# Gate of 16 columns in four column groups, keys first, and new orders in modulated and chunk attention

## Chip, cores and metric

The kernel runs as one program on one core of a Trainium2 chip. The metric is the device time of one execution in microseconds (us), lower is better. Three runs of the kernel before took 3989.94, 3992.09 and 3993.36 us; the median is 3992.09.

## The reference, cut to what matters

The reference is a stack of two layers with layer normalization after each of four sublayers, on 4 x 1024 tokens of 256 features. The change touches two of them. The first attention has 16 heads of 16 features, and a gate per token and head that multiplies the scores:

```python
q = (hidden_states @ Wq + bq)      # 16 heads of 16 features; k and v alike
scores = einsum('bhqd,bhkd->bhqk', q, k) / sqrt(HD)
mod = sigmoid(hidden_states @ cg_W + cg_b + (cons_vec @ am_W + am_b))   # cg_W is 256 x 16
scores = scores * mod.transpose(0, 2, 1)[..., None]
probs = softmax(scores, axis=-1)
```

Beside it a second attention with 4 heads of 64 features is computed from the same tokens (q2, k2, v2). The attention of the second layer works in chunks of 64 tokens: causal softmax attention inside a chunk, plus 0.1 times the queries against a memory matrix per head that earlier chunks have written:

```python
scores = einsum('bhid,bhjd->bhij', qi, ki) * scale      # 16 heads, 64 x 64 a chunk
attn = softmax(where(mask, -inf, scores), axis=-1)
chunk_out = einsum('bhij,bhjd->bhid', attn, vi) + 0.1 * einsum('bhid,bhde->bhie', qi, M)
```

The rest (a third attention, two mixtures of experts, the memory updates) is not touched.

## The kernel before, in words

The stages run one after another, each in a block of its own with one instruction stream per engine: TensorE (PE), VectorE (DVE), ScalarE (ACT), GpSimd (POOL) and SyncE (SP, which issues most transfers). Streams meet only at semaphores. Within a stage the order of each engine is written out by hand.

**First projections**, `project_hidden`. Eight chunks of 512 tokens, two to a pass of the loop (j = 0, 1). The jobs of a chunk are a list: the gate in two tiles of 128 rows, queries and keys in two each, q2 and k2 in two each, values in four. Each job is a product into one of seven PSUM banks, taken in turn; before job n TensorE waits until the bank of job n - 7 has been emptied. For the gate the 16 columns of the weights are repeated 16 times on the host, so that the product has the gate on each of the 256 rows of the queries (`cg_W16`, `am_W16`). ScalarE empties the banks of the gate (L347, sigmoid), the keys (L358), q2 and k2 (L352). VectorE empties the queries with the gate multiplied in (L383), splits queries and keys into three bf16 parts each (`split_exactly`, L206 and L209), and empties the values (L389, L390). SP stores the parts, queries ahead of keys (L295), then q2 and k2 (L299) and the values (L302, L303). GpSimd loads the next tokens (L404). ScalarE issues the loads of the last group of weights before its loop (L188).

**Modulated attention**, `quad_attention`. 16 groups of four heads and one batch, each in two halves of 512 queries, each half in eight units of 128 keys. TensorE computes the scores twice: once ahead (12 units ahead), for the maxima, into a ring of three banks that VectorE reduces (L533, L626), and once for the exponentials (L554), to which the negated maximum is added through rows of the query operand. For that VectorE makes per half a `shift` of two bf16 parts (`make_shift`: L633, L636, L638, each needing the one before), TensorE turns it through a bank of the ring (`turn_shift`, L540), ScalarE copies it (`copy_shift`, L593) and GpSimd places it by transfer (L684). The fourth user after a turn of the same bank waits for the copy. The unit's order on TensorE and ScalarE is

```python
maxima(u + AHEAD, 0); values(u - LAG); maxima(u + AHEAD, 1)
for i in range(2): scores(u, i)
if u in turns: turn_shift(turns[u])          # TensorE
for i in range(2): activation(..., Exp)      # ScalarE, L610
if u in turns: copy_shift(turns[u])
```

`values` (L563) multiplies the exponentials with the values, in four column groups of 32.

**Chunk attention**, `chunk_attention`. 32 tiles of 128 tokens (two chunks), four to an iteration, software-pipelined: at step t TensorE does the scores of tile t (L2561 adds the causal mask, L2565), the output product of tile t - 4 (L2573), the turned probabilities of t - 1 (L2579), the context of t - 2 (L2591 memory part, L2594 values part), and turns the output of t - 8 (L2603). For the scores GpSimd expands the keys (L2539): for each chunk and half of the features eight copies, each blank but for one head's rows. VectorE takes the maximum (L2676), subtracts it (L2678), sums the exponentials of t - 1 (L2668), inverts (L2670) and multiplies (L2673), adds the residual (L2693), takes statistics (L2695, L2697), and once in four tiles writes four tiles of output (L2686). ScalarE takes the exponential (L2623), copies the turned probabilities (L2620), the context (L2628) and the turned output (L2631), and lays out the values (L2639). Expanded keys, scores and probabilities have two buffers each, the turned probabilities one bank pair in PSUM.

## Time and profile before

| | |
|---|---|
| median of three runs | 3992.09 us |
| profiled execution, own time | 3997.91 us |
| its span | 3996.2 us |
| mean granted TensorE clock | 0.938 of full speed |
| TensorE busy | 3580.1 us (90%) |
| VectorE busy | 2339.2 us (59%) |
| ScalarE busy | 1502.5 us (38%) |
| GpSimd busy | 1540.2 us (39%) |
| DMA | 366.44 MB, mean 92 GB/s |

Busy shares are means over stages with different limits. The profile's numbers are of one execution, 5.8 us above the median. A clock of 1.00 is 2.4 GHz, 0.50 is 1.2 GHz. A float32 product shows as two records of its shape. PEld rows are loads of weights, PE rows the products; products are pipelined, so that a row's own time is longer than its distance to the next.

### The profile page before, as it was taken

The numbers are of one execution on the slowest core, as the hardware profiler recorded it, in microseconds if no ns is written. First come the engines' busy times: TensorE is split into PE (matmuls) and PEld (weight loads), VectorE is DVE, ScalarE is ACT, GpSimd is POOL, SyncE is SP. The second block draws the span as 40 slices with busy tenths as digits, with TensorE's granted clock in tenths as the row PEclk, the third lists the DMA queues.
The fourth block names the chain that finished last, engine by engine and source line by source line (L and its number), as shares of the span: only waits on it lengthen the run. The fifth ranks groups of instructions, "written<-read, shape, count | busy, mean of one in ns | idle before, by whom it ended". The sixth has DMA issues, their size and how long they took to land. (4 is left out here: it accounts for less than half of the span.)

```text
span 3996.2 us, 55438 instructions
## 1 busy us (share of the span) xinstructions
PE 3580.1 (90%) x19176; PEld 1710.4 (43%) x19176; DVE 2339.2 (59%) x3916; ACT 1502.5 (38%) x2216; POOL 1540.2 (39%) x1343
## 2 busy tenths in 40 slices
PE   9989999997999889998789656687998989999995
PEld 4412222222333343333545355443554655655653
DVE  5679999994666326664632458977896631111112
ACT  2237777775444323444222334212553211111112
POOL 0142222222788505887346323144552322222221
PEclk9979999998999999999889766899999989999998
DMA  5622222221112151120622421454442123333333
GB/s 182 209 77 68 76 62 62 69 71 48 36 47 63 58 195 58 43 81 16 187 71 85 150 70 45 164 127 109 131 136 83 34 69 91 103 101 105 100 90 95
DMA packets 309775, 366.44 MB, mean 92 GB/s; under 512 B 54130, under 2 KB 241796, under 8 KB 308548
## 3 DMA queue, kind: packets, MB, share of 16 engines
q1 hardware_dynamic: 269972, 305.81, 24.4%
q0 software_dynamic: 30384, 50.90, 5.5%
q10 hardware_dynamic: 9216, 7.09, 0.6%
q8 instruction: 120, 1.97, 0.2%
q14 instruction: 83, 0.68, 0.1%
HBM read 228.00 MB, written 127.27 MB: 89 GB/s over the span
## 5 line engine op out<-in xcount | busy, mean ns | idle before, releaser
L626 DVE TENSOR_REDUCE modulated_mx<-modulated_ring 128x1 f32<-128x512 f32 x1024 | 651.8, 683 | 43.1 <-PE modulated_ring L533 37.4
L610 ACT ACTIVATE modulated_probs<-modulated_scores 128x1024 f32<-128x1024 f32 x512 | 496.1, 1021 | 189.1 <-PE modulated_scores L554 189.0
L3234 DVE TENSOR_TENSOR expert_h<-expert_gelu,expert_bank 128x512 f32<-128x512 f32 x128 | 88.0, 688 | 390.9 <-PE expert_bank L3163 385.4
L3205 ACT ACTIVATE expert_gelu<-expert_bank 128x512 f32<-128x512 f32 x128 | 76.4, 597 | 549.4 <-PE expert_bank L3163 546.5
L3123 POOL DMA_INDIRECT scratch_acc<-expert_y,expert_idx x64 | 100.8, 1575 | 427.5 <-DVE expert_y L3239 404.2
L1019 POOL TENSOR_TENSOR causal_total<-causal_total,causal_probs 128x1024 f32<-128x1024 f32 x96 | 227.1, 2366 | 59.1 <-ACT causal_probs L928 51.7
L1019 POOL TENSOR_TENSOR meta_total<-meta_total,meta_probs 128x1024 f32<-128x1024 f32 x96 | 227.1, 2366 | 58.7 <-ACT meta_probs L928 51.3
L950 DVE TENSOR_REDUCE meta_mx<-meta_maxima 128x2 f32<-128x1024 f32 x120 | 146.9, 1224 | 117.7 <-PE meta_maxima L815 117.1
L950 DVE TENSOR_REDUCE causal_mx<-causal_maxima 128x2 f32<-128x1024 f32 x120 | 146.9, 1224 | 117.7 <-PE causal_maxima L815 117.1
L928 ACT ACTIVATE meta_probs<-meta_scores 128x1024 f32<-128x1024 f32 x128 | 131.0, 1024 | 142.2 <-PE meta_scores L841 139.3
L928 ACT ACTIVATE causal_probs<-causal_scores 128x1024 f32<-128x1024 f32 x128 | 131.0, 1024 | 142.1 <-PE causal_scores L841 139.1
L2539 POOL TENSOR_TENSOR chunk_kexp<-chunk_kT,chunk_blocks 128x512 f32<-128x512 f32 x128 | 138.3, 1112 | 91.8 <-PE chunk_scores L2565 90.9
L563 PE MATMUL modulated_acc<-modulated_probs,modulated_v 128*32 128x512 f32 x1280 | 170.5, 605 | 0.0
L554 PE MATMUL modulated_scores<-modulated_q,modulated_k 128*128 128x512 bf16 x640 | 166.0, 382 | 1.2 <-DMA modulated_q<-modulated_turned 1.2
L1505 PE MATMUL top_ups<-top_wgu,top_xT 128*128 x284 | 142.2, 624 | 2.1 <-ACT top_xT L1553 1.7
L533 PE MATMUL modulated_ring<-modulated_k,modulated_q 64*128 64x512 bf16 x640 | 137.4, 387 | 6.5 <-ACT modulated_turned L593 5.9
L3239 DVE TENSOR_SCALAR expert_y<-expert_bank,chosen_weights 128x256 f32<-128x256 f32 x64 | 31.0, 484 | 188.5 <-PE expert_bank L3160 188.5
L533 PEld LDWEIGHTS modulated_ring<-modulated_k,modulated_q 64*128 64x128 bf16 x640 | 34.2, 92 | 212.5 <-DVE modulated_mx L626 181.7
L3163 PE MATMUL expert_bank<-expert_xT,first_wg 128*128 128x512 f32 x256 | 122.3, 600 | 2.7 <-DVEq L64 1.6
L3163 PE MATMUL expert_bank<-expert_xT,first_wu 128*128 128x512 f32 x256 | 121.4, 597 | 0.0
L3163 PE MATMUL expert_bank<-expert_xT,expert_wg 128*128 128x512 f32 x256 | 120.4, 592 | 1.0 <-DVE expert_h L3234 1.0
L3163 PE MATMUL expert_bank<-expert_xT,expert_wu 128*128 128x512 f32 x256 | 120.3, 592 | 0.0
(546 smaller groups left out, 7521.2 us busy)
## 6 DMA issues: line engine op xcount, KB each, us to landing
scratch_v<-proj_v SPq DMA_DIRECT2D x8, 1024.0 KB, 6.8
ahead_ctx<-scratch_ctx SPq DMA_DIRECT2D x16, 512.0 KB, 4.7
scratch_M<-steps_snap SPq DMA_DIRECT2D x16, 512.0 KB, 3.3
chunk_raw_v<-scratch_v SPq DMA_DIRECT2D x64, 128.0 KB, 2.8
chunk_mem<-scratch_M SPq DMA_DIRECT2D x32, 256.0 KB, 3.0
first_wg<-x_WgT SPq DMA_DIRECT2D x8, 1024.0 KB, 5.0
first_wu<-x_WuT SPq DMA_DIRECT2D x8, 1024.0 KB, 7.1
first_wd<-x_WdT SPq DMA_DIRECT2D x8, 1024.0 KB, 6.8
```

The lines of the kernel that those rows point to most:

```text
L533: nc.tensor.matmul(ring[bank_of["max", 4 * m + j]][:], qs[s][first(j), place(j), t * P:(t + 1) * P], ks[s][first(j), place(j), keys * CH:( ...
L554: last = nc.tensor.matmul(sc[i][:, x, :], ks[s][:, o, t * P:(t + 1) * P], qs[s][:, o, half * CH:(half + 1) * CH], start=True, stop=True)
L563: last = nc.tensor.matmul(acc[32 * j:32 * j + 32, :], vs[g % SLOTS][:, t, j, :], probs[u % NPROBS][j // 2][:, j % 2, :], start=(t == 0), s ...
L610: nc.scalar.activation(probs[u % NPROBS][i][:], sc[i][:], ACT.Exp, scale=SCALE).then_inc(s_exp, 1)
L626: V.tensor_reduce(mx[h % 2][:, x // 2, 1 - j % 2, j // 2, x % 2:x % 2 + 1], ring[bank_of["max", 4 * m + j]][:], AX.X, ALU.max).then_inc(s_ ...
L928: nc.scalar.activation(probs[u % NPROBS][:], sc[u % 2][:], ACT.Exp, scale=SCALE).then_inc(s_exp, 1)
L950: V.tensor_reduce(mx[g % 2][:, x // 2, :, x % 2], maxima_at(m)[:], AX.X, ALU.max).then_inc(s_red, 1)
L1019: G.tensor_tensor(total[g % 2][:], total[g % 2][:], probs[u % NPROBS][:], ALU.add).then_inc(s_add, 1)
L1505: last = nc.tensor.matmul(ups[i % 2][:], xT[i % 2][:, kd, :], wgu[:, kd, bass.ds(e, 1), :].rearrange("p e n -> p (e n)"), start=(kd == 0), ...
L2539: ins = G.tensor_tensor(kexp[j % 2][:, c, h], kT[j][:, h, c * C64:(c + 1) * C64].unsqueeze(1).broadcast_to([P, HP, C64]), blocks[:].unsque ...
L3123: added[j].done(G.indirect_dma_start(out=scr["acc"], out_offset=bass.IndirectOffsetOnAxis(ap=idx[j][a][:], axis=0), in_=y[j][:, a, :], in_ ...
L3163: last = nc.tensor.matmul(out[:], (wg if kind == "g" else wu)[j][:, kd, m * P:(m + 1) * P], xT[j][:, kd, :], start=(kd == 0), stop=(kd == ...
```

## The change

In the projections the gate becomes one job a chunk, on 32 columns (the 16 twice): four column groups of the array each take a quarter of the chunk's 512 tokens. ScalarE takes one sigmoid of 128 x 128 and issues eight transfers that lay each head's row on the 16 rows of its features. The keys come ahead of the queries.

```diff
-        T_KINDS = ("mod", "q", "k", "q2", "k2")
+        T_KINDS = ("k", "q", "q2", "k2")
+        GROUPS, WIDE = 4, P // 4
...
-        kinds = [(x, m) for x in T_KINDS for m in range(KD)] + [("v", t) for t in range(TT)]
+        kinds = [("gate", 0)] + [(x, m) for x in T_KINDS for m in range(KD)] + [("v", t) for t in range(TT)]
...
+                    if kind == "gate":
+                        for kd in range(KD):
+                            for r in range(GROUPS):
+                                toks = slice(r * (CH // GROUPS), (r + 1) * (CH // GROUPS))
+                                last = nc.tensor.matmul(bank[n % BANKS][r * WIDE:(r + 1) * WIDE, 0:CH // GROUPS], wg[:, kd, :], xT[j][:, kd, toks],
+                                                        start=(kd == 0), stop=(kd == KD - 1))
...
-                    if kind == "mod":
-                        dve_s.wait(act, i, (1 - j, "q", m), back=1 - j)
-                        ins = nc.scalar.activation(mod[:, m, :], bank[n % BANKS][:], ACT.Sigmoid, bias=modb[:, m:m + 1])
+                    if kind == "gate":
...
+                        act_s.done(nc.scalar.activation(gate[:], bank[n % BANKS][:, 0:CH // GROUPS], ACT.Sigmoid, bias=modb[:]), job)
+                        act_s.wait(act, i, job)
+                        dve_s.wait(act, i, (1 - j, "q", KD - 1), back=1 - j)
+                        for r in range(GROUPS):
+                            for c in range(KD):
+                                first = r * WIDE + c * (P // HD16)
+                                mod_laid[j].done(act.dma_start(mod[:, c, r * (CH // GROUPS):(r + 1) * (CH // GROUPS)],
+                                                               gate[first:first + P // HD16, :].unsqueeze(1).broadcast_to([P // HD16, HD16, CH // GROUPS])))
+                        continue
...
-                        act_s.wait(dve, i, (j, "mod", m))
+                        if m == 0:
+                            mod_laid[j].wait(dve, i)
```

In modulated attention the turned shift goes ahead of the unit's scores on TensorE, its copy ahead of the exponentials on ScalarE, and the three operations of `make_shift` go between the reductions of the unit that follows.

```diff
+                if u in turns:
+                    turn_shift(turns[u])
                 for i in range(2):
                     scores(u, i)
-                if u in turns:
-                    turn_shift(turns[u])
...
+                if u in turns:
+                    copy_shift(turns[u])
                 for i in range(2):
                     act.wait_ge(s_sc, 2 * u + i + 1)
...
-                if u in turns:
-                    copy_shift(turns[u])
...
+                    made_here = m % KT == 0 and before > 0
+                    reduce(m, range(0, 1))
+                    if made_here:
+                        lowest(before)
+                    reduce(m, range(1, 2))
+                    if made_here:
+                        shift_high(before)
+                    reduce(m, range(2, Q))
+                    if made_here:
+                        shift_rest(before)
```

In chunk attention the expanded keys hold four heads' blocks instead of eight, and each score product uses 64 of the rows; the memory parts of the context come ahead of all values parts; GpSimd normalizes the probabilities; TensorE turns them last in a step; ScalarE takes the exponential ahead of the copy of the turned probabilities.

```diff
-                        for c in range(2):
-                            for h in range(HH):
-                                ins = G.tensor_tensor(kexp[j % 2][:, c, h], kT[j][:, h, c * C64:(c + 1) * C64].unsqueeze(1).broadcast_to([P, HP, C64]),
-                                                      blocks[:].unsqueeze(2).broadcast_to([P, HP, C64]), ALU.mult)
+                        for h in range(HH):
+                            ins = G.tensor_tensor(kexp[j % 2][:, h], kT[j][:, h, :].rearrange("p (c k) -> p c k", c=2).unsqueeze(2).broadcast_to([P, 2, QUAD, C64]),
+                                                  own[:].unsqueeze(1).unsqueeze(3).broadcast_to([P, 2, QUAD, C64]), ALU.mult)
                         pool_k.done(ins)
+                    if live(at, j, 1):
+                        o = (j - 1) % 2
+                        dve_rec.wait(pool, t - 1)
+                        pe_turn.wait(pool, t - 3)
+                        pool_normed.done(G.tensor_tensor(normed[o][:], probs[o][:], rec[o][:].unsqueeze(2).broadcast_to([P, H16, C64]), ALU.mult))
...
-                                last = nc.tensor.matmul(sc[c * C64:(c + 1) * C64, h * HP:(h + 1) * HP, :].rearrange("p h k -> p (h k)"),
-                                                        qT[j][:, h, c * C64:(c + 1) * C64], kexp[j % 2][:, c, h].rearrange("p h k -> p (h k)"),
-                                                        start=False, stop=True, skip_group_check=True)
+                                for r in range(ROWS):
+                                    at_rows = slice(r * C64, (r + 1) * C64)
+                                    last = nc.tensor.matmul(sc[c * C64:(c + 1) * C64, r * HP + h * QUAD:r * HP + (h + 1) * QUAD, :].rearrange("p a k -> p (a k)"),
+                                                            qT[j][at_rows, h, c * C64:(c + 1) * C64], kexp[j % 2][at_rows, h, c].rearrange("p a k -> p (a k)"),
+                                                            start=False, stop=True, skip_group_check=True)
...
+                        for c, h, toks in both:
+                            nc.tensor.matmul(ctxps[:, h, toks], mem[m][:, c, h * P:(h + 1) * P], qT[m][:, h, toks],
+                                             start=(c + h == 0), stop=False, skip_group_check=True)
+                        for c, h, toks in both:
+                            for r in range(PAIRS // HH):
+                                last = nc.tensor.matmul(ctxps[32 * r:32 * r + 32, h, toks], val[m][:, c, h * (PAIRS // HH) + r, :],
+                                                        probsT[m % 2][:, r // 2 * QUAD + h * 2 + r % 2, toks], start=False, stop=True, skip_group_check=True)
...
+            V.tensor_reduce(own[:], blocks[:].rearrange("p (a b) -> p b a", b=QUAD), AX.X, ALU.add).then_inc(s_own, 1)
...
-                        dve_rec.wait(dve, t - 1)
-                        pe_turn.wait(dve, t - 3)
-                        dve_normed.done(V.tensor_tensor(normed[o][:], probs[o][:], heads(rec[o]), ALU.mult))
```

The bias of the gate is made with three small products instead of six, and the host lays out `cg_W2`, `am_W8`, `cg_b8` and `am_b8` in place of the repeated arrays.

## Rows read from the trace of the kernel before

**Rows 1.** The timeline of TensorE in the projections: start, us, what.
```profile
36.51 3.60 PE L330 MATMUL proj_bank<-proj_xT,proj_w_mod 128*128 128x512 f32 x8
39.95 0.59 PE L330 MATMUL proj_bank<-proj_xT,proj_w_q 128*128 128x512 f32 x1
```

**Rows 2.** The timeline of weight loads in modulated attention; brackets: idle before, releaser.
```profile
507.22 0.10 PEld L533 LDWEIGHTS modulated_ring<-heads_k,heads_q 64*128 64x128 bf16 x2 [0.84 <-DVE modulated_mx L626]
...
509.83 0.09 PEld L533 LDWEIGHTS modulated_ring<-heads_k,heads_q 64*128 64x128 bf16 x1 [0.84 <-DVE modulated_mx L626]
...
512.85 0.10 PEld L533 LDWEIGHTS modulated_ring<-heads_k,heads_q 64*128 64x128 bf16 x2 [0.84 <-DVE modulated_mx L626]
...
516.30 0.10 PEld L533 LDWEIGHTS modulated_ring<-heads_k,heads_q 64*128 64x128 bf16 x2 [1.20 <-ACT modulated_turned L593]
```

**Rows 3.** The timeline of TensorE in chunk attention.
```profile
2830.79 1.84 PE L2579 MATMUL chunk_turned<-chunk_ident,chunk_pnorm 128*128 128x128 f32 x8 [2.21 <-DVE chunk_pnorm L2673]
...
2914.91 1.94 PE L2565 MATMUL chunk_scores<-chunk_kexp,chunk_qT 128*64 128x512 f32 x8
...
2921.77 1.94 PE L2565 MATMUL chunk_scores<-chunk_kexp,chunk_qT 128*64 128x512 f32 x8
...
2925.98 1.09 PE L2579 MATMUL chunk_turned<-chunk_ident,chunk_pnorm 128*128 128x128 f32 x8 [1.21 <-DVE chunk_pnorm L2673]
...
2927.17 0.32 PE L2594 MATMUL chunk_ctx_and_new_turned<-chunk_probsT,chunk_val 128*32 128x64 f32 x8
...
2927.42 0.43 PE L2591 MATMUL chunk_ctx_and_new_turned<-chunk_qT,chunk_mem 128*128 128x64 f32 x2
...
2930.07 1.08 PE L2565 MATMUL chunk_scores<-chunk_kexp,chunk_qT 128*64 128x512 f32 x4
```

**Rows 4.** Groups of instructions: busy us, mean ns of one, idle before and releasers.
```profile
L2686 DVE TENSOR_SCALAR chunk_new<-chunk_y,chunk_mv,chunk_inv 128x256 f32<-128x256 f32 x32 | 15.5, 546 | 1.4 <-DVE chunk_inv L2681 1.3
...
L2539 POOL TENSOR_TENSOR chunk_kexp<-chunk_kT,chunk_blocks 128x512 f32<-128x512 f32 x128 | 138.3, 1112 | 91.8 <-PE chunk_scores L2565 90.9 <-DMA chunk_kT<-scratch_kT 0.9
...
L1019 POOL TENSOR_TENSOR causal_total<-causal_total,causal_probs 128x1024 f32<-128x1024 f32 x96 | 227.1, 2366 | 59.1 <-ACT causal_probs L928 51.7
...
L2623 ACT ACTIVATE chunk_probs<-chunk_s 128x1024 f32<-128x1024 f32 x32 | 33.8, 1057 | 2.1 <-DVE chunk_s L2678 1.5
```

**Rows 5.** Windows of chunk attention: PE, PEld, DVE, ACT, POOL busy, clock, DMA.
```profile
2903.00:3018.00 115.00, 106.39 (x1005) 67.18 (x1004) 100.31 (x154) 62.17 (x105) 51.71 (x48) 1.00 0.38 116
2831.00:2841.00 10.00, 10.00 (x60) 5.43 (x58) 5.73 (x8) 3.57 (x6) 1.64 (x2) 0.50 0.29 93
```

**Rows 6.** The timeline of the projections: an issue in ScalarE's queue.
```profile
9.23 0.49 ACTq L188 DMA_DIRECT2D proj_b_q<-L_attn_ca_bin  x1
```

**Rows 7.** Groups of instructions of the projections.
```profile
L347 ACT ACT_TABLE_LOAD x4 | 5.1, 1283 | 37.6 <-PE proj_bank L330 37.6
...
L383 DVE SCALAR_TENSOR_TENSOR proj_q_full<-proj_bank,proj_b_q,proj_mod 128x512 f32<-128x512 f32 x16 | 12.0, 748 | 39.2 <-PE proj_bank L330 39.2
...
L206 DVE CAST proj_k_part<-proj_rest 128x512 bf16<-128x512 f32 x32 | 13.7, 427 | 1.1
...
L209 DVE TENSOR_TENSOR proj_rest<-proj_k_full,proj_k_part 128x512 f32<-128x512 f32 x16 | 11.1, 692 | 0.5
```

**Rows 8.** DMA issues of 0 to 215 us: KB each, median us to landing.
```profile
scratch_v<-proj_v SPq DMA_DIRECT2D x8, 512.0 KB, 7.7
```

**Rows 9.** The timeline of ScalarE in modulated attention.
```profile
505.58 1.94 ACT L610 ACTIVATE modulated_probs<-modulated_scores 128x1024 f32<-128x1024 f32 x2 [0.67 <-PE modulated_scores L554]
```

**Rows 10.** The timeline of VectorE in chunk attention.
```profile
2993.87 1.22 DVE L2668 TENSOR_REDUCE chunk_sums<-chunk_probs 128x16 f32<-128x1024 f32 x1 [0.38 <-ACT chunk_probs L2623]
...
2995.41 1.22 DVE L2673 TENSOR_TENSOR chunk_pnorm<-chunk_probs,chunk_rec 128x1024 f32<-128x1024 f32 x1
2996.68 1.23 DVE L2676 TENSOR_REDUCE chunk_mx<-chunk_scores 128x16 f32<-128x1024 f32 x1
...
3000.74 1.22 DVE L2668 TENSOR_REDUCE chunk_sums<-chunk_probs 128x16 f32<-128x1024 f32 x1 [0.25 <-ACT chunk_probs L2623]
```

122 lines of the change are left out of this document (68 added, 54 removed).

## The prediction

> **What bounds the kernel now.** I read the windows first, by stage, then the groups of instructions, the waits, and a short stretch of the timeline in each stage that the diff touches: the first projections (about 10 to 206 us), modulated attention (212 to 969) and chunk attention (2755 to 3020). The other 2,780 us run the same code. In each of the three the reader is to see which engine has no gap.
>
> Projections: TensorE goes through without a pause. Eight records of the gate's matrix take 36.51 to 39.95, 3.44 us, and the next group follows at once [rows 1]. A chunk is seven such lengths, 24.1 us, and there are eight chunks.
>
> Modulated attention: the weight loads of the maxima show the step. A plain unit (two pairs of maxima, scores, values) is 507.22 to 509.83, 2.61 us. The next, with VectorE's three small operations for the shift in it, is 3.02, and the one with the turned shift 3.45, where the last pair waited 1.20 us for ScalarE's copy [rows 2]. So one half (8 units) carries 0.41 + 0.84 = 1.25 us beyond 8 x 2.61, 32 times.
>
> Chunk attention: one tile is 2914.91 to 2921.77, 6.86 us, with TensorE unbroken; the next is 8.30, with a wait of 1.21 for VectorE's normed probabilities [rows 3]. That is once in four tiles, where VectorE also writes four tiles of output, 4 x 0.546 = 2.2 us [rows 4]. Four tiles are 3 x 6.86 + 8.30 = 28.9 us. In 2903 to 3018 TensorE is busy 106 and VectorE 100 of 115 us [rows 5]: both are near their limit.
>
> **The change, part by part.** *A, the gate.* Removed: eight records a chunk, 3.44 us. Added: 16 records, 32 columns wide, with 128 columns of data, on four column groups. No row has this shape. The nearest is the values product of chunk attention, also 32 wide on four column groups: eight records with 64 columns take 2927.17 to 2927.42, 0.25 us, change of shape included [rows 3]. Twice the records and twice the columns make 0.5 to 1.0; I take 0.7. From above, a 512-column record costs 3.44 / 8 = 0.43, so 128 columns one after another cost 16 x 0.107 = 1.7. A chunk saves 2.7 (1.7 to 2.9), eight save 22.
>
> What lies beside it: ScalarE now issues eight transfers a chunk. An issue there takes 0.49 [rows 6], so about 4.2 us, behind a table load of 1.28 in every second chunk and a sigmoid over 128 columns, shorter than the 0.75 of VectorE's pass over 512 [rows 7]. Queued behind them on ScalarE are the two passes that empty the keys' banks. VectorE waits for these, and the transfers themselves hold back only its first query pass. Counted from the gate's start: keys emptied at about 7.6, VectorE splits them in 2 x (3 x 0.43 + 2 x 0.69) = 5.4 and comes to the queries at 13. The last transfer is issued at 6.9. A store of 512 KB takes 7.7 us to land beside other traffic [rows 8]; the 64 KB pieces at that price would be there at 14.6, at half of it at 11. The second query bank must be free when TensorE comes to the job seven further on, at 0.7 + 10 x 1.72 = 17.9. With queries begun at 13 it is free at 13 + 0.75 + 2.7 + 0.75 = 17.2. So the transfers cost nothing as long as the key splits cover them; when that cover is gone, TensorE stands 0.5 to 1 us a chunk. SP sends the query parts ahead of the key parts as before; the finished key parts wait there some 3 us, and the next chunk needs their buffer only 6 us after that. I take 2 us off for all this: **A is -20**, between -8 (1.7 saved and 0.7 of standing a chunk) and -24. Smaller weights and three fewer bias products at the start are worth about 1 us, inside that.
>
> *B, modulated attention.* The three small operations go between reductions, where their results are not waited for; of the 0.41 us I take 0.3 back. The turned shift goes ahead of the scores. It then waits for the reduction two places back, some 0.2 us, and puts the scores 0.5 later; what it gives back is ScalarE's copy, now ahead of the exponentials, so the wait of 1.20 goes. The exponentials queued behind the copy start 0.7 later, but ScalarE is idle 0.67 before each pair of them [rows 9]. What is late next is the first pair of maxima of the following unit: 0.47 against the 0.84 of today. Gain 0.3 + 0.4 = 0.7 a half, 32 halves: **B is -22**. If the small operations gain nothing and the turn only 0.25, -8; if all of the 1.25 goes but 0.22 for the turn's own matmuls, -33.
>
> *C, chunk attention.* Scores: 8 records with 512 columns become 16 with 256, in quadrants. Today they take 1.87. With only pairs beside each other that stays; with all four it is half. Context: the four changes between the 128-wide and the 32-wide products become one. Today a quarter costs 2927.17 to 2927.42 and the pair of memory records before it, 0.61 in all; I take 1.7 for 2.46. TensorE's tile falls from 6.86 to 5.2 (6.1 at the worst). GpSimd gives up two of four expansions (each 1.112, so 4.4 becomes 2.2) and takes the normed probabilities from VectorE: 1.27 from its start to the next there [rows 10], 2.37 for a 128x1024 product on GpSimd [rows 4]. Together 4.6, as now.
>
> TensorE is then no longer the end. The chain is: expanded keys 2.2, scores 1.6 and 0.2 to arrive, maximum and subtraction 2.45 (1.23 each), exponential 1.06 and 0.1, sums and reciprocal 1.54, normed 2.4 [rows 4, 10]. It closes over two tiles, because GpSimd expands the keys of tile t after it has normed tile t-2: 11.6 us. The four output tiles (2.2, and the 0.2 before them) lie in one of the two such chains of an iteration. VectorE alone needs 5.3 for a plain tile (2993.87 to 3000.74, less 0.25 of waiting and 1.27 for the product [rows 10]) and 7.7 for one with output. Laid one after another (7.7, then 14.0 from the start, 19.3, 25.6), four tiles take 25.6 us against 28.9; 7 full iterations save 23. The first and last tiles gain and lose about 1 each. `own_of_four` adds one VectorE pass before the loop, under the wait for the first memory transfer.
>
> Against it stands the clock. In 2831 to 2841 the granted clock was 0.50, that is 1.2 GHz [rows 5], after TensorE had stood 2.21 us; after the 1.21 at 2925.98 it did not fall [rows 3]. Now it will stand 1 to 2.5 us in every iteration. Ten us at the lower level are 5 us of matrix work lost, of which the idle time takes back one or two: a fall costs 3 to 4. I allow one more than today's two: **C is -20**. With a fall in each of seven iterations it is +5; with VectorE alone as the end (3 x 5.3 + 7.7 = 23.6 an iteration) and no new fall it is -34.
>
> GpSimd's price deserves a second look. The row says 2.37 for the product on GpSimd, and keys that took 1.11 on average. The Trainium skill, GPSIMD Engine Reference, section Key points, says that GpSimd contends with VectorE's instructions that read two SBUF tensors, and that VectorE is about twice as fast elementwise; by the first the expansions get quicker once VectorE's product is gone, by the second the move is a loss. The rows bear out the second (1.27 against 2.37), no row isolates the first; by a GpSimd product without contention C would gain about 3 us more.
>
> Sum: -20 - 22 - 20 = -62. The profiled execution took 3997.9 (its span of 3996.2 and 1.7 around it), 5.8 above the median of 3992.1. From it the sum gives 3936, from the median **3930**.
>
> **Rivals.** (1) The clock and the chain eat the gain of C. For: TensorE is given 1 to 2 us of idleness a tile. Against: the stretch 2903 to 3018 kept 1.00 with such waits. A and B stay: 3992 - 42 = 3950. (2) All goes as well as the bounds allow: quadrants fully beside each other, copies never waited for, -24 - 33 - 34: 3901. (3) Nothing is gained: transfers land late and TensorE stands in A, the turn's wait costs what the copy did, the chain in C is as long as today: 3990. Against: all three would have to fail. (4) Slower: chunk attention runs at the lower clock as a whole. Its place is TensorE's idle time between the turned probabilities and the next scores. TensorE's 5.2 us a tile become 10.4; 32 tiles cost 333 against 231 us today, +102, with A and B +60: 4052. It decides from the point where each iteration begins with a fall and the clock doesn't return before the next. Against it: today it returned after 10 us.
>
> A rule would make (2) stronger: the Trainium skill, TensorEngine Tiling (Array Packing), section Theoretical Speedup, gives up to 2x for each of the two small dimensions, so four 64x64 tiles at once. Today's scores already run two abreast (1.87 us for eight records of 0.43 each). By that rule scores take 0.95, which is what my 5.2 contains; by the row alone they stay at 1.87, C's hop is 12.5 and C gains 10 us less.
>
> **Chances.** Forecast 0.58, (1) 0.20, (2) 0.12, (3) 0.06, (4) 0.04. Range 3898 to 3968: it takes in (1) and nearly (2), with A and C at their worst beside B's middle above. A measurement of this kernel can tell about 0.2% (8 us) from no change; faster by more 0.90 (forecast, (1) and (2)), within it 0.06 ((3)), slower 0.04 ((4)).
>
> **What would show it.** A: the gate's 16 records within 1 us, no gap in TensorE's projections, VectorE's first query pass not waiting for a transfer, the stage 20 us shorter. B: the wait of the maxima for the copy gone, a half of 21.4 instead of 22.1 us. C: scores under 1.2 us, an iteration near 25.6 us, TensorE waiting for GpSimd's keys, normed products of 2.4 us on GpSimd. I am wrong if TensorE's gap before the queries' banks opens, if the half stays above 22, or if the granted clock of chunk attention is below 0.9.

## The result, and the profile after

The changed kernel takes 3975.2 us (median of 9 runs, 3973.0 to 3981.6) against 3989.9 for the one before in the same comparison: a ratio of 0.9964, with a 95% interval of 0.9955 to 0.9973. That is faster by 15 us where I forecast 62, and outside my range of 3898 to 3968. The two attention parts paid more than I said; the gate, to which I had given the narrowest bounds, cost 51 us.

Where the time lies in the profiled executions, us; the attention stages by their first and last instruction, GpSimd's left out:

| | before | after | forecast | measured |
|---|---|---|---|---|
| first projections, to the start of modulated attention | 212.2 | 263.1 | -20 | +50.9 |
| modulated attention | 750.3 | 725.6 | -22 | -24.7 |
| chunk attention | 263.0 | 217.4 | -20 | -45.6 |
| causal attention (not touched) | 390.2 | 386.7 | 0 | -3.5 |
| span | 3996.2 | 3971.4 | | -24.8 |

The spans differ by 24.8 and the medians by 15: the profiled execution of before (3997.9) lay 8 us above its median, that of after (3973.1) 2 us below.

**First projections.** The timeline of TensorE (start, us, what, idle before and its releaser), the answer to [rows 1]:

```profile
88.86 1.98 PE L341 MATMUL proj_bank<-proj_wv,proj_xT 128*128 128x512 f32 x4 [0.81 <-DVE proj_q_full L408]
92.35 3.70 PE L341 MATMUL proj_bank<-proj_wv,proj_xT 128*128 128x512 f32 x8 [1.51 <-DVE proj_q_full L408]
95.98 0.64 PE L332 MATMUL proj_bank<-proj_xT,proj_wg 128*32 128x128 f32 x16
96.56 1.98 PE L341 MATMUL proj_bank<-proj_xT,proj_w_k 128*128 128x512 f32 x4
...
113.96 3.40 PE L341 MATMUL proj_bank<-proj_xT,proj_w_k 128*128 128x512 f32 x4 [5.12 <-ACT proj_k_full L382]
```

The gate's 16 records take 0.58 us (95.98 to 96.56), against the 3.44 that went. In the kernel without transfers (e6 below) a chunk takes 21.37 us against 24.03, so the change saves 2.66 a chunk in matrix work, and I had said 2.7. But TensorE, which had no gap before, now stands in each chunk: longest (5.12) ahead of the second tile of k2, the first job that needs the bank of the keys again, then shorter ahead of the values. Who is late is in the waits of the whole stage (engine, tile, line, releaser: us in total, times, longest):

```profile
DVE proj_k_part L206 <- ACT proj_k_full L382: 121.2, 8, 16.2
ACT proj_k_full L382 <- issue: 111.8, 8, 16.1
...
PEld proj_bank L341 <- ACT proj_k_full L382: 37.5, 7, 5.9
PEld proj_bank L341 <- DVE proj_q_full L408: 32.2, 16, 3.8
PE proj_bank L341 <- ACT proj_k_full L382: 31.7, 7, 5.1
PE proj_bank L341 <- DVE proj_q_full L408: 19.5, 14, 3.0
```

In the 8 chunks ScalarE empties the keys' bank 14 us late on average, and what it did meanwhile is "issue": the eight transfers. TensorE itself stands 31.7 + 19.5 = 51.2 us. The tile's own rows say what one costs (issue ns min/median/max, then VectorE's wait for the landing):

```profile
L369 ACTq DMA_DIRECT2D proj_mod<-proj_gate x64: 611/1791/3348, 13.0 to 235.2; - x64
...
  DMA proj_mod<-proj_gate: 2.0, 1
```

I had 0.49 for one, from a small load [rows 6]. The shortest is 0.61 and the median 1.79. The eight of the first chunk take 6.9 us from first to last, those of the other seven chunks 13.9 to 15.7; there, too, the first of the eight takes only 0.61 to 0.64. The windows show the difference (PE, PEld, DVE, ACT, POOL busy, granted clock, DMA share, GB/s): the first chunk; a later one; and the same one, behind the stand of 5.12.

```profile
14.00:20.00 6.00, 6.00 (x14) 2.50 (x14) 0.00 (x0) 0.00 (x0) 0.00 (x0) 1.00 0.37 71
97.00:109.00 12.00, 11.84 (x28) 4.94 (x26) 0.79 (x3) 0.14 (x1) 0.44 (x1) 1.00 0.98 321
114.00:116.00 2.00, 2.00 (x3) 0.97 (x4) 1.90 (x4) 2.00 (x4) 0.00 (x0) 0.50 0.17 23
```

In the later chunks the stores of the chunk just finished and the load of the next fill all the DMA engines just then. The third window shows a second price: behind each long stand the granted clock was 0.50 for some 3 us (7 in the last chunk), after TensorE had stood for 3.9 to 5.1 us, and work at that level cost about 12 us over the stage by a sum over windows of 1 us. Part A of the prediction had no term for the clock. SyncE's own issues of these stores are slow there too, where the same ones took 0.37 us each in before (timeline of its queue in after):

```profile
99.60 2.54 SPq L306 DMA_DIRECT2D scratch_v<-proj_v  x1
102.33 2.46 SPq L307 DMA_DIRECT2D scratch_v<-proj_v  x1
```

**Modulated attention.** The weight loads around one turned shift, the answer to [rows 2]:

```profile
553.45 0.10 PEld L558 LDWEIGHTS modulated_ring<-heads_k,heads_q 64*128 64x128 bf16 x2 [0.84 <-DVE modulated_mx L651]
554.01 0.24 PEld L565 LDWEIGHTS modulated_ring<-modulated_ident,modulated_shift 128*128 128x128 bf16 x4 [0.46 <-issue]
...
555.21 0.10 PEld L558 LDWEIGHTS modulated_ring<-heads_k,heads_q 64*128 64x128 bf16 x2 [0.42 <-DVE modulated_mx L651]
...
556.54 0.10 PEld L558 LDWEIGHTS modulated_ring<-heads_k,heads_q 64*128 64x128 bf16 x2 [0.84 <-issue]
```

The unit with the turn takes 3.09 us (553.45 to 556.54) where it took 3.45, and the wait of 1.20 for the copy is gone. The distance of two turns, a half, fell from 22.13 to 21.35 us.

**Chunk attention.** TensorE's timeline of one tile, the answer to [rows 3]:

```profile
2905.44 1.09 PE L2619 MATMUL chunk_scores<-chunk_kexp,chunk_qT 64*64 64x256 f32 x16
2906.47 1.13 PE L2627 MATMUL chunk_out<-chunk_wo,chunk_ctxT 128*128 128x256 f32 x4
2907.44 1.00 PE L2638 MATMUL chunk_ctx_and_new_turned<-chunk_qT,chunk_mem 128*128 128x64 f32 x8
2908.37 0.65 PE L2642 MATMUL chunk_ctx_and_new_turned<-chunk_probsT,chunk_val 128*32 128x64 f32 x32
2910.56 0.44 PE L2651 MATMUL chunk_ctx_and_new_turned<-chunk_ident,chunk_new 128*128 128x128 f32 x2 [1.54 <-DVE chunk_new L2740]
```

GpSimd's two groups of instructions (busy us, mean ns, idle before and releasers), for [rows 4]:

```profile
L2586 POOL TENSOR_TENSOR chunk_kexp<-chunk_kT,chunk_own_of_four 128x512 f32<-128x512 f32 x54 | 55.1, 1042 | 0.0
L2593 POOL TENSOR_TENSOR chunk_pnorm<-chunk_probs,chunk_rec 128x1024 f32<-128x1024 f32 x26 | 49.4, 1902 | 55.7 <-DVE chunk_rec L2727 51.8 <-PE chunk_scores L2619 3.9
```

And the window of 160 us, for [rows 5]:

```profile
2800.00:2960.00 160.00, 139.92 (x1903) 103.64 (x1903) 140.27 (x214) 101.18 (x169) 103.30 (x80) 0.99 0.55 167
```

Scores take 1.03 us (1.87 before), context 1.5, an iteration of four tiles 24.3 (28.9 before; I forecast 25.6), and the granted clock stayed at 0.99 over 160 us.

### The profile page after: what moved, and what is told of

Same layout as the page of the kernel before. It is cut to its first block and busy times, and to the rows that moved or that the text cites. A ratio compares the mean times of both kernels' runs of the same rounds, so it can differ in the third digit from the quotient of the medians.

```text
span 3971.4 us, 56116 instructions
## 1 busy us (share of the span) xinstructions
PE 3504.1 (88%) x19490; PEld 1686.5 (42%) x19490; DVE 2283.2 (57%) x3885; ACT 1486.2 (37%) x2208; POOL 1524.4 (38%) x1311
## 5 line engine op out<-in xcount | busy, mean ns | idle before, releaser
L1063 POOL TENSOR_TENSOR meta_total<-meta_total,meta_probs 128x1024 f32<-128x1024 f32 x96 | 227.1, 2365 | 58.7 <-ACT meta_probs L972 51.2
L558 PE MATMUL modulated_ring<-modulated_k,modulated_q 64*128 64x512 bf16 x640 | 124.9, 386 | 0.0
L3214 PE MATMUL expert_bank<-expert_wd,expert_h 128*128 128x256 f32 x512 | 111.9, 379 | 1.2 <-DVEq L64 1.2
```

Source lines behind the costliest of these rows:

```text
L558: nc.tensor.matmul(ring[bank_of["max", 4 * m + j]][:], qs[s][first(j), place(j), t * P:(t + 1) * P], ks[s][first(j), place(j), keys * CH:( ...
L1063: G.tensor_tensor(total[g % 2][:], total[g % 2][:], probs[u % NPROBS][:], ALU.add).then_inc(s_add, 1)
L3214: last = nc.tensor.matmul(out[:, 0:D], h[j][:, f, m * P:(m + 1) * P], wd[j][:, f, :], start=(f == 0), stop=(f == FT - 1))
```

## The experiments

All sixteen in one table; stages in us from the profiled executions, the kernel's time as median, a ratio to before with its interval where it was timed in rounds, else one time. Only the stage that an edit touches is shown.

| kernel | stage | its length | time | ratio to before |
|---|---|---|---|---|
| before / after | projections | 204.6 / 252.0 | 3989.9 / 3975.2 | 0.9964 (0.9955-0.9973) |
| e1 old gate | projections | 205.2 | 3920.4 | 0.9822 (0.9809-0.9836) |
| e2 gate spread by TensorE | projections | 207.3 | 3928.3 | 0.9838 (0.9825-0.9852) |
| e3 issues on GpSimd | projections | 219.4 | 3941.5 | 0.9874 (0.9859-0.9889) |
| e4 issues after keys | projections | 229.4 | 3953.3 | 0.9904 (0.9889-0.9919) |
| e5 queries last | projections | 198.5 | 3920.4 | 0.9827 (0.9813-0.9840) |
| e6 no transfers | projections | 180.6 | 3896.7 | |
| e7 quarter of the bytes | projections | 226.0 | 3953.3 | |
| e8 two gates | projections | 191.9 | 3916.8 | 0.9810 (0.9797-0.9824) |
| e9 half the descriptors | projections | 242.6 | 3963.0 | |
| e12 two long, GpSimd | projections | 208.9 | 3933.0 | 0.9864 (0.9847-0.9880) |
| e13 two long, ScalarE | projections | 243.6 | 3966.0 | 0.9944 (0.9927-0.9960) |
| e15 gate ahead | projections | 182.8 | 3901.1 | 0.9772 (0.9759-0.9786) |
| e10 product on VectorE | chunk | 248.4 | 3955.0 | |
| e11 old orders | chunk | 260.9 | 3967.8 | |
| e14 scores in whole rows | chunk | 270.0 | 3977.8 | |
| e16 quadrants alone | chunk | 252.3 | 3956.5 | |

**e1: the old gate, the new attention stages.**

```diff
-        T_KINDS = ("k", "q", "q2", "k2")
+        T_KINDS = ("mod", "q", "k", "q2", "k2")
```

> The projections of the kernel before, with the new orders of both attention stages. Theory 1 (the loss lies wholly inside the first projections: the eight issues stand on ScalarE's queue ahead of the keys): the stage goes back from 252.0 to 204.6 us, the modulated stage begins near 212 us, and the kernel takes the time after less 50.9, about 3924 us. Rival (the new attention stages gave 45.6 and 24.8 us only because something in the new projections helps them, or are worth less alone): above 3945 us.

3920.4 us, and the stage at 205.2. So the loss lies inside the first projections, and B and C are worth 70 us by themselves. That is more than I gave the whole change.

**e3: the issues on GpSimd; e4: on ScalarE, behind the keys.**

```diff
+                    act_s.wait(pool, i, (j, "gate", 0))
...
-                                mod_laid[j].done(act.dma_start(mod[:, c, r * (CH // GROUPS):(r + 1) * (CH // GROUPS)],
+                            mod_laid[j].done(pool.dma_start(mod[:, c, r * (CH // GROUPS):(r + 1) * (CH // GROUPS)],
```

> The same eight transfers a chunk, issued by GpSimd, which has only the load of the hidden states in this stage. Theory 1 (their place on ScalarE's queue is what costs): no stand of TensorE behind the keys, stage about 180 to 190 us, kernel 3900 to 3910 us. Theory 2 (the transfers themselves are what costs, landing late in the crowd of stores): VectorE waits for them at the first query for several us in each of the 8 chunks, stage above 220 us, kernel above 3940 us.

> The same eight transfers on ScalarE, but issued after the keys' two activations and ahead of q2's. Theory 1: the keys' splits run at once and cover the issues; what is left is that q2's and k2's banks are emptied up to 14 us late, which 7 banks hide in part: stage 205 to 230 us, kernel 3930 to 3950 us. Theory 2 (the transfers cost wherever they are issued): stage 245 us or more and the kernel at 3970 us or more.

e3 took 219.4 us, between the theories but at the edge of theory 2; e4 took 229.4, at the slow end of what theory 1 allowed. The waits of e3 show why:

```profile
DVE proj_q_full L397 <- DMA proj_mod<-proj_gate: 62.1, 8, 9.1
...
PEld proj_bank L341 <- DVE proj_q_full L397: 37.2, 15, 4.4
...
DVE proj_k_part L206 <- ACT proj_k_full L371: 15.5, 5, 5.4
```

The keys' wait fell from 121 to 15.5 us: the place on the queue was one cost. But a second stood behind it, which in the changed kernel had cost 2.0 us in all: the transfers land late, and VectorE waits 62 us for them at the queries. While the keys were 14 us late, nobody could see that. In e4 VectorE's wait for the landing is 71.5 us. The eight issues take 4.7 to 5.4 us in every chunk on GpSimd, against 13.9 to 15.7 on ScalarE.

**e5: queries last.** On e3, with the order k, q2, k2, q and SyncE's stores likewise.

```diff
-        T_KINDS = ("k", "q", "q2", "k2")
+        T_KINDS = ("k", "q2", "k2", "q")
```

> The eight transfers issued by GpSimd, and the queries moved behind the second keys: gate, k, q2, k2, q, v, with SyncE's stores in that order. With the issues on GpSimd in the old place the keys no longer waited (121 us became 15.5) but VectorE waited 62 us for the transfers at the first query, 7.8 a chunk, and the stage took 219.4 us. Theory (two costs: the place on the queue, and a landing that comes later than the keys cover): four more tiles of TensorE work, 6.9 us, lie ahead of the first query, so nearly all of the 62 us goes: stage 185 to 195 us, kernel 3893 to 3903 us. Rival (the landing slips with whatever stores run beside it, or VectorE, whose work now bunches behind the queries, holds TensorE's banks): stage 205 us or more, kernel above 3915 us.

198.5 us, between the two, with 46.7 us of waiting for the transfers left. I put this down to the single buffer of the laid-out gate, since the queries that read it now end a chunk and the next chunk's transfers may be issued only behind them. The next version with two buffers (e8) says otherwise. The stage is 6.7 us shorter than in e1, yet the two medians are equal; intervals of 0.3% leave open which is the faster.

**e6: no transfers.**

```diff
-                        for r in range(GROUPS):
-                            for c in range(KD):
-                                first = r * WIDE + c * (P // HD16)
-                                mod_laid[j].done(act.dma_start(...
+            nc.vector.memset(mod[:], 1.0)
```

> The narrow gate is computed and put through the sigmoid, but never laid out: the eight transfers are left out and the queries are multiplied by ones, so the output differs in the gate. What the gate's matmuls are worth by themselves. If TensorE alone sets the stage: 204.6 less 8 x 2.86, so 182 us, and the kernel 3905 us. If VectorE or the stores set it as soon as TensorE is shorter: 195 us or more, kernel above 3918 us.

180.6 us: TensorE alone sets the stage (no gap in it), and the narrow gate is worth 24 us when nothing need be laid out. So my -22 for the matrix work was right, and everything else is the price of the transfers: 71 us as the change makes them, of which TensorE stood 51 and about 12 are the lower clock behind the stands. The kernel leaves the layout out, so its output differs.

**e7: a quarter of the bytes; e9: half the descriptors (and with them half the bytes).**

```diff
-                                mod_laid[j].done(act.dma_start(mod[:, c, r * (CH // GROUPS):(r + 1) * (CH // GROUPS)],
+                                mod_laid[j].done(act.dma_start(mod[:, c, r * (CH // GROUPS):r * (CH // GROUPS) + 32],
```

```diff
-                                mod_laid[j].done(act.dma_start(mod[:, c, r * (CH // GROUPS):(r + 1) * (CH // GROUPS)],
+                                mod_laid[j].done(act.dma_start(mod[0:P // 2, c, r * (CH // GROUPS):(r + 1) * (CH // GROUPS)],
```

> The changed kernel with transfers of 32 of the 128 tokens: the same eight issues and the same 128 descriptors each, of 128 bytes in place of 512, so three quarters of the gate stay ones in the output. If an issue is slow by what it issues (its descriptors), the eight still take 14 to 16 us a chunk and the stage stays near 250 us. If it is slow because the transfer's bytes cannot leave in the crowd of stores, they fall to about 0.6 us each, some 5 us a chunk, and the stage to 200 to 215 us, the kernel to 3925 to 3940 us.

> The changed kernel with transfers of 4 heads in place of 8: eight issues on ScalarE as before, each of 64 descriptors of 512 bytes (half the descriptors and half the bytes), the other half of the gate's rows stay ones in the output. With a quarter of the bytes and all the descriptors the issues took a median of 1.41 us. If the count of descriptors is what an issue waits on, half of them bring the eight to 7 us or less a chunk and the stage to 215 us or less; if the bytes count, they take 9 to 11 us and the stage 225 to 235 us.

Neither is the whole cause. The stage takes 226.0 us with a quarter of the bytes, between my two values, and 242.6 with half the descriptors, above both of mine, against 252.0. From the first issue to the last of a chunk it takes 10.1 to 12.2 us with a quarter of the bytes (5.8 in the first chunk) and 12.0 to 15.2 with half the descriptors (6.7 in the first), against 13.9 to 15.7 (6.9). The chunk without stores beside it is the one that differs, in all three kernels. Fewer bytes buy some of it; the larger part comes, by elimination, from the crowd of stores and the load. The runs don't show by which mechanism it holds ScalarE's issues and not GpSimd's, nor why the first issue of each eight stays short.

**e8: two gates.** On e5, with a second gate and a second laid-out gate.

```diff
-        mod = st.sb("mod", [P, KD, CH])
+        mod = [st.sb(f"mod{j}", [P, KD, CH]) for j in range(2)]
```

> As the kernel with the queries last and the issues on GpSimd, with a second gate and a second laid-out gate in memory. There the transfers of one chunk could not be issued before the last queries of the chunk ahead had read the single buffer (GpSimd waited 121 us for VectorE), and VectorE then waited 46.7 us for them. Theory (the buffer, then the landing): issued right behind the sigmoid, some 12 us before the first query, they land in time; VectorE's wait for them is under 10 us in all, the stage 182 to 188 us against 180.6 without any transfer, the kernel 3900 to 3907 us. Rival (the transfers' bytes crowd the stores and loads, so that something else lands late): stage 192 us or more, kernel 3912 us or more.

191.9 us, the edge of the rival, and still 46.5 us of waiting, against 46.7 with one buffer. So the buffer was not what held the transfers: in e5 as in e8 the first issue comes 1.9 or 3.1 us behind the gate's start in every chunk but the first (3.1 where ScalarE loads its table). The last of the eight lands 11.2 to 16.4 us behind the first issue, a single one up to 11.7 behind its own. Half of the 6.6 us gained lies in the last chunk; what the buffer did there is open. Also the start of modulated attention lies 10.7 us behind the stage's last instruction instead of 6.5; I put that down to the last stores, which is not shown.

**e12, e13: two long transfers.** The gate with each head eight times over 128 columns, laid out by two transfers of 256 KB.

```diff
+                        for c in range(KD):
+                            mod_laid[j].done(act.dma_start(mod[:, c, :], gate[c * (P // HD16):(c + 1) * (P // HD16), :].unsqueeze(1).broadcast_to([P // HD16, HD16, CH])))
```

> The gate as one tile of 128 columns over all 512 tokens (each head eight times; 4 records of 0.43 us where the old gate had 8), laid out by two transfers of 256 KB whose descriptors are 2 KB (8 heads x 16 copies, 256 a chunk in place of 1,024 of 512 bytes), issued by GpSimd. TensorE's work is 1.72 us a chunk less than before. Theory D (the short descriptors fill the DMA engines: 93 to 112 GB/s at a share of 0.9 while they ran, 340 to 380 GB/s for the stores): the long ones land within some 4 us, ahead of the first query, and the stage takes 204.6 - 8 x 1.72, about 191 us; the kernel 3904 to 3910 us. Rival (a transfer of this stage lands 8 us or more behind its issue whatever its descriptors, because of the stores ahead of it): VectorE waits 3 us or more at the first query of each chunk, stage 205 us or more, kernel 3920 us or more.

> The same two long transfers issued by ScalarE, ahead of the keys, as the change has its eight. Theory Q (the cost is issues times what one waits): two issues of 0.6 to 1.5 us, up to 3 us ahead of the keys, covered by VectorE's slack: stage 190 to 200 us, kernel 3905 to 3918 us. Rival (an issue on ScalarE waits for room for its bytes, 256 KB each now): the two take as long as the eight, 14 to 16 us, stage near 250 us.

Theory D fell and its rival held: 208.9 us. On GpSimd's queue the two transfers need 7.2 and 7.4 us in the first chunk with nothing beside them, and there they fill the DMA engines:

```profile
18.00:22.00 4.00, 4.00 (x11) 1.83 (x10) 3.09 (x7) 0.36 (x1) 0.00 (x0) 1.00 0.97 95
```

A share of 0.97 at 95 GB/s, where the window with the stores makes 321 at 0.98. In later chunks they land 9.4 to 14.7 us behind their issue. On ScalarE the two issues are cheap as theory Q said (1.3 to 2.5 us), yet the stage takes 243.6, outside both of my ranges: the landing is most of the cost, as the waits of e13 say.

```profile
DVE proj_q_full L402 <- DMA proj_mod<-proj_gate: 67.9, 8, 12.4
```

Six us behind the last store's issue, with what I take to be only these transfers still under way, the window of e13 shows the DMA engines half used:

```profile
106.00:110.00 4.00, 3.94 (x10) 1.43 (x8) 0.00 (x0) 1.37 (x2) 0.00 (x0) 1.00 0.50 78
```

That half has a rule beside it: the Trainium skill, DMA: Bandwidth & Descriptors, section Rules for kernel authors, says that a transfer whose outermost dimension is smaller than 16 runs on at most that many engines. Here the outermost dimension is 8 heads, and the share of 0.50 on ScalarE's queue agrees. On GpSimd's queue 0.97 was reached, so there the rule did not show.

**e2: the gate spread by TensorE.**

```diff
+                    if kind == "lay":
...
+                        mm.done(nc.tensor.matmul(bank[n % BANKS][:], spread[:, m * P:(m + 1) * P], gate[:], start=True, stop=True), job)
```

> The gate narrow, but laid on the heads' rows by TensorE instead of by transfers: two records of 512 columns for 16 heads, ScalarE's sigmoid over 16 rows, two more records against a matrix of ones and zeros that spread it over 256 rows, and ScalarE copies those two banks. Four records of 0.43 us stand where eight stood (3.44 us a chunk), so 1.7 us a chunk less than before and nothing issued. Theory 1: stage about 204.6 - 14 = 191 us, kernel 3910 us. Rival (the chain matmul, sigmoid, matmul, copy is not hidden by the keys, or VectorE and not TensorE sets the chunk): stage 204 us or more, kernel 3924 us or more.

3928.3 us, slower than e1. My sum was wrong by a factor of two: two products of 512 columns are four records each way, so eight stand where eight stood, as the groups say.

```profile
L336 PE MATMUL proj_bank<-proj_xT,proj_wg 128*16 128x512 f32 x32 | 16.8, 652 | 1.6 <-DMA proj_xT<-hT 1.6
L332 PE MATMUL proj_bank<-proj_gate,proj_spread 16*128 16x512 f32 x32 | 15.8, 613 | 0.0
```

A chunk takes 24.7 us against 24.0. The matrix work has no gap in either; each group behind a change of tile shape takes 0.1 to 0.2 us more than the same number of records before, which makes up the rest.

**e15: the gate of every second chunk ahead of the values before it.** On e8.

```diff
+        jobs = [(0, "gate", 0)] + [(0, *x) for x in kinds[:at_v]] + [(1, "gate", 0)] + [(0, *x) for x in kinds[at_v:]] + [(1, *x) for x in kinds]
```

> As the kernel with two gates and the queries last, with the gate of every second chunk computed ahead of the chunk before's values, 7 us of TensorE work earlier; the transfers of it are issued then. In the kernel with two gates the transfers landed up to 11.7 us behind their issue, VectorE waited 46.5 us for them over 7 chunks, and the stage took 191.9 us against 180.6 with no transfers. Theory (a landing of 10 to 12 us that only more work ahead of the first query can hide): half of the chunks lose their wait, 20 to 25 us stay, the stage takes 185 to 188 us, the kernel 3908 to 3913 us. Rival (the DMA engines' time itself is short now, so that earlier transfers only push the stores and loads back): stage 190 us or more, kernel 3915 us or more.

182.8 us and 3901.1: better than forecast, within 2.2 us of the stage without any transfer, and 0.5% faster than e1. It is the best version of this study, 1.9% faster than the changed kernel. VectorE still waits 30.4 us for the transfers, in four chunks, without TensorE standing for it. TensorE has no gap left (window of 120 us):

```profile
60.00:180.00 120.00, 120.00 (x352) 52.79 (x352) 81.72 (x167) 27.79 (x41) 43.61 (x74) 1.00 0.90 251
```

**Chunk attention: e10, e11, e14, e16.** All on e1. e10 puts the product of probabilities and inverse sums back on VectorE. e11 puts the copy of the turned probabilities and TensorE's turns back in their old places. e14 puts the scores back into whole rows. e16 has the edits of e10 and e11 together, so that the quadrants stand alone with the regrouped context, which no run takes back. The diffs are those of e10, e11 (TensorE's part) and e14.

```diff
-                        pool_normed.done(G.tensor_tensor(normed[o][:], probs[o][:], rec[o][:].unsqueeze(2).broadcast_to([P, H16, C64]), ALU.mult))
+                        dve_normed.done(V.tensor_tensor(normed[o][:], probs[o][:], heads(rec[o]), ALU.mult))
```

```diff
+                    if live(at, j, 1):
+                        pool_normed.wait(pe, t - 1)
...
                     if live(at, j, 2):
...
-                    if live(at, j, 1):
-                        pool_normed.wait(pe, t - 1)
```

```diff
-                                for r in range(ROWS):
...
-                                                            qT[j][at_rows, h, c * C64:(c + 1) * C64], kexp[j % 2][at_rows, h, c].rearrange("p a k -> p (a k)"),
+                                                        qT[j][:, h, c * C64:(c + 1) * C64], kexp[j % 2][:, c, h].rearrange("p h k -> p (h k)"),
```

> The kernel with the old gate and the new attention orders, and in chunk attention the product of probabilities and inverse sums back on VectorE (1.31 us a tile). Theory V (VectorE set the chunk stage: 6.65 us of work in 7.2 us a tile before, 5.35 in 6.05 now): the 32 tiles give back about 1.2 us each, the stage goes from 215.5 to 250 to 258 us, and nearly all of the stage's gain is gone. Theory T (TensorE's shorter scores and shorter chain made the gain, as I forecast): under 230 us.

> The same kernel with ScalarE's copy of the turned probabilities ahead of the exponentials again, and TensorE's turns ahead of the context again; the product stays on GpSimd, the scores in quadrants. Theory V: the orders matter only by the room they leave GpSimd's product: in the old place TensorE's turns come 1 to 2 us too early for it, stage 225 to 240 us. Rival (the orders are free once VectorE is lighter): under 219 us.

> The kernel with the old gate and the new attention orders, with chunk attention's scores in the old form (128 rows, 8 heads each, zeros in the other heads' rows; GpSimd's four products of 1.1 us a tile instead of two of 1.04). Theory of a shared bound: GpSimd then has 4.4 + 1.9 = 6.3 us a tile where a tile takes 6.05, and TensorE 0.84 us more: stage 225 to 235 us. Theory V alone (VectorE sets it): under 220 us. Theory T (the shorter scores made most of the gain): 240 us or more.

> Old gate, new modulated attention, and of chunk attention's edits only the quadrants (shorter scores, GpSimd's two products of keys in place of four) with the regrouped context: the product back on VectorE and both orders as before. With one part of the three taken back each time the stage took 248.4, 260.9 and 270.0 us, with all three 215.5, with none 263.0. If the parts only pay together (VectorE's product is the bound again): 250 to 262 us. If shorter scores pay by themselves, 0.84 us a tile: 236 to 242 us.

Theory V held for e10 (248.4, just under its range), and for e16 (252.3) the expectation that the parts only pay together. For e11 (260.9) both values were far too low. For e14 (270.0) only theory T allowed so much, but TensorE is busy 116 of 140 us there, so it isn't full. The windows of 140 us, in the order e1, e10, e11, e14, columns as above:

```profile
2780.00:2920.00 140.00, 121.93 (x1641) 89.71 (x1631) 124.60 (x198) 92.02 (x155) 89.93 (x71) 1.00 0.57 170
```

```profile
2780.00:2920.00 140.00, 115.28 (x1416) 83.69 (x1416) 129.89 (x187) 76.35 (x131) 45.56 (x39) 0.89 0.48 144
```

```profile
2780.00:2920.00 140.00, 111.91 (x1367) 79.54 (x1366) 103.92 (x163) 77.01 (x126) 74.31 (x57) 0.93 0.47 141
```

```profile
2780.00:2920.00 140.00, 115.86 (x1194) 72.48 (x1193) 100.28 (x157) 71.05 (x119) 109.13 (x94) 0.98 0.47 138
```

With the product on VectorE, VectorE is busy 93% of the window: 6.5 us of work in a tile of 7.0. With the old orders no engine is full: the chain is. TensorE's queue holds the turns ahead of the context, and they wait for GpSimd's product (timeline of e11), with everything behind them:

```profile
2856.39 1.09 PE L2608 MATMUL chunk_turned<-chunk_ident,chunk_pnorm 128*128 128x128 f32 x8 [1.35 <-POOL chunk_pnorm L2568]
...
2864.65 1.72 PE L2608 MATMUL chunk_turned<-chunk_ident,chunk_pnorm 128*128 128x128 f32 x8 [2.86 <-POOL chunk_pnorm L2568]
```

With whole rows GpSimd has 6.1 us a tile, four products of keys and one of probabilities, and a tile takes 7.6 on average; TensorE waits 16.7 us of the 140 for the keys and VectorE 33.7 for the scores, so I read the chain through GpSimd as the bound there. The clock has a share in all of these: 0.89, 0.93 and 0.98 against 1.00. Taken away singly from the full set, the product costs 33 us, the orders (two edits, not parted) 45 and the quadrants 55; together they gained 47.5. Quadrants alone gain 11 (263.0 to 252.3). So most of the gain belongs to the combination, and none of the three has one price.

## Why the prediction was wrong

**The step that failed** is in part A: "ScalarE now issues eight transfers a chunk. An issue there takes 0.49 [rows 6], so about 4.2 us". It took 6.9 us in the first chunk and 13.9 to 15.7 in the others. The row was one small load at the start of the kernel, with the DMA engines idle; the issues of the change fall where the finished chunk's stores and the next load run at a share of 0.98. From it came "keys emptied at about 7.6": some 18 us in truth, and I had named these two passes as queued behind. Two stands follow from that. TensorE comes to the second tile of k2, which needs the first keys' bank, at 0.7 + 7 x 1.72 = 12.7, and it is free at about 18: the 5.1 us, for which my sum had no line. And with 10 more microseconds in my own sum the second query bank is free at 27 instead of 17.2, against the 17.9 at which TensorE needs it. The lower clock behind each stand, a term that I had put at nothing in A, made it worse. A later chunk grew from 24.0 to between 30 and 33 us. Rival (3) named a stand of TensorE in A, but for the landing and not for the issues.

**The second step**, "the 64 KB pieces at that price would be there at 14.6, at half of it at 11", was hidden in the changed kernel and comes to light in e3, e5, e8 and e13. In e3 the last of the eight landed 16.5 to 19.0 us behind the gate's start in the later chunks (13.9 in the first), and the first query waited 7.4 to 9.1 for it. I priced the landing by a store [rows 8]; a copy from 8 rows of memory to 128 moves 95 GB/s at a full share (e12).

**Point by point.** The gate's 16 records: 0.58, forecast 0.7. The gate without its layout: -24, forecast -22. "VectorE's first query pass not waiting for a transfer": true (2.0 us), and for the wrong reason. B: -24.7, forecast -22; a half of 21.35, forecast 21.4. Of the 0.41 of the small operations all came back, not 0.3: the units beside the turn take 2.61 us. The turn still costs 0.48 (3.09 less 2.61), the 0.47 forecast. C: -45.6, forecast -20. Scores took 1.03 us, under my 1.2. By the rule cited there (the Trainium skill, TensorEngine Tiling (Array Packing), section Theoretical Speedup) the estimate was 0.95; the trace agrees within 0.1, and the row by itself would have given 1.87. Context about 1.5, forecast 1.7. GpSimd's product is 1.90 us, not 2.37; the row I took has two full operands, this one a broadcast factor, and no run shows whether that is the reason. The keys' products take 1.04 instead of 1.11 on the mean, and 1.20 and 1.32 in e10 and e16. The mean hides two kinds: in e10 the 43 of 64 that run beside no product of VectorE take 1.04, of the other 21 the longest 2.08. The trace of before could have told me: 99 of 128 ran apart from VectorE's product and took 1.05 on the mean, 29 ran beside it and took up to 2.03. It is the contention that the Trainium skill names (GPSIMD Engine Reference, section Key points), and these runs agree.

The two together shorten my chain of 11.6 to 11.0, and with that my own laying out gives 7.7, 13.4, 18.7 and 24.4 us. The steps measured between VectorE's maxima are 7.5, 13.3, 18.5 and 24.3: the chain was built right and GpSimd's two prices in it were too high. Of the -45.6, the seven full iterations make 39.3, where I had 23. Five give 3.3 to 4.8 each, 21.3 in all. The third and the fifth give 9.8 and 8.2: in before they took 34.2 and 32.6, with a granted clock of 0.50 (2831 to 2841) and 0.83 (2890 to 2910) in them, and now they take 24.4. I had charged 3 us for one more fall of the clock instead of striking out these two. The first and last tiles gave the other 6.3, for which I had nothing. The clock stayed at 0.99 over 160 us (0.91 in one stretch of 20), so rivals (1) and (4) had nothing to stand on.

Rival (2), 3901, is the time of e15, but by luck: its parts were -24, -33 and -34, and those of e15 are about -22, -25 and -45.

**The sum.** With A at +51, B at -25 and C at -46 the steps explain -19 of the profiled -25. Another -3.5 is causal attention, which takes 390.2 us in before, 389.8 in e1 and 386.5 to 386.7 in after, e10 and e15 without an edit there. It arises in the stage's first 45 us: from 20 to 40 us behind its start the granted clock was 0.91 in before and 0.93 in e1, and 1.00 in after and e10. Why it came back later there is open.

## What to carry to other kernels

An issue on a compute engine's queue is work of that engine: price it in the traffic in which it will fall, and put it on an engine that nobody waits for. A small layout made by transfers needs a lead of more than its landing time ahead of its reader, or as much slack behind it; moving the producer earlier gave that in e15, and then nearly all of the matrix work saved was really saved. A wait of an engine also has a price behind it where the clock falls, so count both. When two delays lie beside each other, removing the longer shows the other, so measure the edit with the layout left out (here 180.6 us) to know what is to be had.

## What was not expected of the hardware

- Eight issues on ScalarE's queue take 5.8 to 6.9 us in the first chunk, with no stores beside them, and 13.9 to 15.7 beside the stores; behind the keys (e4) they take 10.4 to 14.9, with a quarter of the bytes 10.1 to 12.2. On GpSimd's queue they take 4.7 to 5.5 in all traffic.
- Copies from 8 rows of on-chip memory to 128 run at 95 GB/s with the DMA engines at a share of 0.97 when GpSimd issues them, and at 78 GB/s with a share of 0.50 when ScalarE does; the window with the stores out of 128 rows makes 321 at 0.98.
- A product of 128x1024 with one broadcast operand takes GpSimd 1.90 us, with two full ones 2.37 [rows 4]; its 128x512 products take 1.04 us, and up to 2.08 where VectorE multiplies probabilities and inverse sums beside them (e10).
